# Seven scattered result areas replaced by two accumulating ones in a mixture-of-experts decoder layer

## The reference

```
N, k = 4096, 1024
scores = softmax(xt @ Wr)                      # token x expert
G, idx = top_k(scores.T, k)                    # each expert picks 1024 tokens
X_in = xt[idx]
h = gelu(einsum('ekd,edh->ekh', X_in, W1) + b1)
X_e = einsum('ekh,ehd->ekd', h, W2) + b2
contrib = G[..., None] * X_e
out = zeros((N, D)).at[idx].add(contrib)       # a token may be picked by several experts
x = layernorm(x + out)
```

## Time and profile before

| | |
|---|---|
| median of 3 runs | 586.69 us (585.83 to 591.93) |
| profiled execution | span 585.1 us, 11240 instructions (no time of its own is given beside the span) |
| TensorE busy | 94% of the span |
| VectorE, ScalarE, GpSimd busy | 71%, 56%, 44% |
| mean granted TensorE clock | 0.977 of full |
| HBM read, written | 36.85 MB, 26.08 MB |

### The profile page before, as it was taken

How to read it: one execution, slowest core, us unless ns; L and a number is a source line. 1 busy time by engine, 2 the same in 40 slices (tenths; PEclk the granted TensorE clock), 3 DMA queues, 4 the chain that set the end, 5 groups by cost and what they waited for, 6 DMA issues and landing times.

```text
span 585.1 us, 11240 instructions
## 1 busy us (share of the span) xinstructions
PE 549.5 (94%) x3477; PEld 427.6 (73%) x3477; DVE 417.1 (71%) x1051; ACT 327.3 (56%) x670; POOL 260.2 (44%) x368
## 2 busy tenths in 40 slices
PE   8999999999999999999999898998999999999880
PEld 7868787888888788788878676566676575668530
DVE  3686786787687688668877875788758845656753
ACT  3577776767777677776767543442333525443133
POOL 4123524434352443435243430002777777777732
PEclk9999999999999999999999998998999999999985
DMA  7033442232234023423312404900223443665652
GB/s 242 2 82 91 135 117 52 96 109 97 47 115 134 25 83 115 112 50 115 104 60 65 150 10 144 304 2 11 55 57 106 138 129 121 191 194 163 221 185 108
DMA packets 62151, 63.43 MB, mean 108 GB/s; under 512 B 11809, under 2 KB 48930, under 8 KB 61858
## 3 DMA queue, kind: packets, MB, share of 16 engines
q1 hardware_dynamic: 58096, 55.37, 30.8%
q0 software_dynamic: 3584, 7.58, 4.6%
q10 hardware_dynamic: 434, 0.02, 0.0%
HBM read 36.85 MB, written 26.08 MB: 108 GB/s over the span
## 4 chain that ended last, share of the span: by engine, by line
PE 77%; DVE 13%; ACT 4%; issue 2%; POOL 1%; DMA 1%; POOLq 0%; DVEq 0%; ACTq 0%
PE PS L1577 17%; PE PS L1635 10%; PE PS L1607 9%; PE PS L1908 8%; PE PS L1930 7%; PE PS L1623 5%; PE PS L1821 4%; PE PS L1831 4%; DVE pc L1395 2%; DVE csum L1158 1%; ACT shared L891 1%; DVE cmax L1147 1%; PE PS L1681 1%; PE PS L1675 1%; PE PS L1667 1%
## 5 line engine op out<-in xcount | busy, mean ns | idle before, releaser
L767 POOL TENSOR_TENSOR pn<-pc,crcp 128x512 f32<-128x512 f32 (+1 forms) x93 | 80.4, 891 | 69.3 <-DVE crcp L1161 69.3
L1035 ACT ACTIVATE shared<-PS,b1T 128x512 f32<-128x512 f32 x88 | 60.5, 687 | 85.7 <-PE PS L1821 49.5
L807 POOL DMA_INDIRECT shared<-table,idx x56 | 54.3, 970 | 64.5 <-DVE idx L1402 48.0
L1607 PE MATMUL PS<-shared,x1T 128*128 128x512 f32 (+1 forms) x192 | 72.4, 513 | 1.2 <-ACT x1T L906 1.0
L817 POOL DMA_INDIRECT spread<-pn,idx x56 | 62.0, 1107 | 17.6 <-issue 15.6
L1607 PEld LDWEIGHTS PS<-shared,x1T 128*128 128x128 f32 x192 | 35.0, 189 | 37.6 <-issue 35.2
L862 ACT ACTIVATE shared<-PS 128x308 f32<-128x308 f32 x120 | 47.5, 428 | 25.5 <-PE PS L1577 25.2
L1147 DVE TENSOR_REDUCE cmax<-PS 128x16 f32<-128x1232 f32 x31 | 44.7, 1441 | 20.8 <-PE PS L1607 20.4
L1158 DVE TENSOR_REDUCE csum<-pc 128x16 f32<-128x1232 f32 x31 | 44.4, 1431 | 19.4 <-ACT pc L874 19.4
L1908 PE MATMUL PS<-pT,w 128*128 128x512 f32 x112 | 53.6, 611 | 3.3 <-ACT pT L1030 3.3
L1930 PEld LDWEIGHTS PS<-w,shared 128*128 128x128 f32 x448 | 51.7, 192 | 3.6 <-issue 3.1
(11 more groups left out here) (209 smaller groups left out, 1208.1 us busy)
## 6 DMA issues: line engine op xcount, KB each, us to landing
spread<-zeros SPq DMA_DIRECT2D x112, 128.0 KB, 2.0
shared<-spread SPq DMA_DIRECT2D x56, 256.0 KB, 4.3
xboth<-in_x SPq DMA_DIRECT2D x16, 256.0 KB, 2.7
w<-in_W SPq DMA_DIRECT2D x2, 1792.0 KB, 9.2
rest<-stage SPq DMA_DIRECT2D x56, 52.0 KB
table<-x SPq DMA_DIRECT2D x16, 128.0 KB, 1.9
fin<-table SPq DMA_DIRECT2D x1, 2048.0 KB, 18.2
out_x<-fin SPq DMA_DIRECT2D x8, 256.0 KB, 2.0
```

The lines of the kernel that those rows point to most:

```text
L767: pool.tensor_tensor(pn[:, e, at_pn:at_pn + n * (b - a)].rearrange("p (h k) -> p h k", h=n), pc[:, e, :].rearrange("p (h k) -> p h k", h=H ...
L807: pool.indirect_dma_start(xg[:, e % 3, h, :], None, table, bass.IndirectOffsetOnAxis(ap=idx[:, e, h:h + 1], axis=0)).then_inc(gathered[e % ...
L1035: act.activation(hid[:, c, 512 * h:512 * h + 512], PS[:, HID_BANKS[k % len(HID_BANKS)], :], ACT.Gelu, bias=b1T[:, bias:bias + 1]).then_inc ...
L1607: i = pe.matmul(PS[:, n, 0:b - a], x1T[:, e, :], A[:, 2 * A_SLOT[phase] + e, a:b], start=True, stop=True)
```

## The change

Only two HBM areas remain, `spread[0]` and `spread[1]`. Even experts scatter to the first and odd ones to the second. Experts 0 and 1 overwrite cleared rows, as before; experts 2 to 6 use indirect DMAs that add to what the area holds (`compute_op=ALU.add`), and GpSimd waits before them until the scatters of expert e - 2, which went to the same area, have landed. SP clears two areas and loads two: `spread[1]` after the scatters of experts 1, 3 and 5, and `spread[0]` after those of 0, 2, 4 and 6, each part of it after the add of the same part of the first. VectorE adds eight parts, after `last_results`, in place of 48; TensorE takes in the second area by its identity matmuls.

```diff
+AREAS = 2
-        spread = [nc.dram_tensor(f"spread{e}", ...).ap() for e in range(LISTED)]
+        spread = [nc.dram_tensor(f"spread{e}", ...).ap() for e in range(AREAS)]
             def clear(q):
-                for e in range(LISTED):
+                for e in range(AREAS):
                     sp.dma_start(to_clear[e][q], zeros[:, :]).then_inc(cleared, 16)
...
-            for e in range(LISTED):
+            for e in range(LISTED - AREAS, LISTED):
                 sp.wait_ge(scattered[e % 2], 16 * SB * (e // 2 + 1))
-                rows = spread[e].rearrange("(t b) d -> t b d", t=P)
+                rows = spread[e % 2].rearrange("(t b) d -> t b d", t=P)
                 for c in range(B // 4):
-                    if e:
-                        sp.wait_ge(landed_added, B // 4 * (e - 1) + c + 1)
+                    if e == LISTED - 1:
+                        sp.wait_ge(landed_added, c + 1)
                     sp.dma_start(landed[:, 4 * c:4 * c + 4, :], rows[:, 4 * c:4 * c + 4, :]).then_inc(landed_in[c], 16)
...
             def scatter(e):
                 if e == 0:
-                    pool.wait_ge(cleared, 16 * LISTED * PAIRS)
+                    pool.wait_ge(cleared, 16 * AREAS * PAIRS)
+                if e >= AREAS:
+                    pool.wait_ge(scattered[e % 2], 16 * SB * (e // 2))
                 for h in range(SB):
                     pool.wait_ge(ye_done, blocks_through(e, h))
-                    pool.indirect_dma_start(spread[e], bass.IndirectOffsetOnAxis(ap=idx[:, e, h:h + 1], axis=0),
-                                            ye[:, e % 2, h, :], None).then_inc(scattered[e % 2], 16)
+                    rows = bass.IndirectOffsetOnAxis(ap=idx[:, e, h:h + 1], axis=0)
+                    if e < AREAS:
+                        pool.indirect_dma_start(spread[e % 2], rows, ye[:, e % 2, h, :], None).then_inc(scattered[e % 2], 16)
+                    else:
+                        pool.indirect_dma_start(spread[e % 2], rows, ye[:, e % 2, h, :], None,
+                                                compute_op=ALU.add).then_inc(scattered[e % 2], 16)
...
-            def dense_add(g, landed_before):
+            def dense_add(g):
-                if landed_before:
-                    dve.wait_ge(landed_added, landed_before)
...
-            def add_landed(e, first, last):
-                if e == 0 and first == 0:
-                    dve.wait_ge(fin_x, 16)
-                if added[0]:
-                    dve.wait_ge(dense_added, added[0])
-                for c in range(first, last):
-                    dve.wait_ge(landed_in[c], 16 * (e + 1))
-                    if e:
-                        dve.wait_ge(landed_added, B // 4 * (e - 1) + c + 1)
+            def add_landed():
+                dve.wait_ge(dense_added, added[0])
+                for c in range(B // 4):
+                    dve.wait_ge(landed_in[c], 16)
                     dve.tensor_tensor(fin[:, 4 * c:4 * c + 4, :], fin[:, 4 * c:4 * c + 4, :],
                                       landed[:, 4 * c:4 * c + 4, :], ALU.add).then_inc(landed_added, 1)
...
                 results(e, 0)
-                if e >= 2:
-                    add_landed(e - 2, 0, B // 8)
                 results(e, 1)
-                if e >= 2:
-                    add_landed(e - 2, B // 8, B // 4)
...
-            add_landed(LISTED - 3, 0, B // 4)
             last_results()
-            add_landed(LISTED - 2, 0, B // 4)
+            add_landed()
```

More of the change, by code:

```diff
@@ L456, in decoder_layer @@
         table = nc.dram_tensor("table", [TOKENS, ROW], F32, kind="Internal").ap()
-        spread = [nc.dram_tensor(f"spread{e}", [TOKENS, P], F32, kind="Internal").ap() for e in range(LISTED)]
+        spread = [nc.dram_tensor(f"spread{e}", [TOKENS, P], F32, kind="Internal").ap() for e in range(AREAS)]
         rest = nc.dram_tensor("rest", [PAIRS // PHASES, 2 * PHASES, HEADS, KEYS_REST, P], F32, kind="Internal").ap()
@@ L1479, in _ @@
                     make_idx(e + 3)
-                if e >= 2:
-                    add_landed(e - 2, 0, B // 8)
                 results(e, 1)
-                if e >= 2:
-                    add_landed(e - 2, B // 8, B // 4)
                 if e < 2:
                     for k in range(IN_ROUTING // 2 * e, IN_ROUTING // 2 * (e + 1)):
-                        dense_add(k, 0)
+                        dense_add(k)
                 if e - 1 in TAIL:
-                    dense_add(TAIL[e - 1], B // 4 * (e - 1))
-            add_landed(LISTED - 3, 0, B // 4)
+                    dense_add(TAIL[e - 1])
             last_results()
-            add_landed(LISTED - 2, 0, B // 4)
+            add_landed()
             def fin_shift(c):
@@ L1500, in fin_shift @@
                                          in1=rsf[:, 4 * c:4 * c + 4], op0=ALU.mult, op1=ALU.mult).then_inc(fin_shifted, 1)
-            dve.wait_ge(landed_added, B // 4 * (LISTED - 1))
+            dve.wait_ge(landed_added, B // 4)
             for c in range(B // 4):
@@ L1976, in _ @@
             for c in range(B // 4):
-                pe.wait_ge(landed_added, B // 4 * (LISTED - 2) + c + 1)
+                pe.wait_ge(landed_added, c + 1)
                 pe.matmul(PS[:, c, :], ident[:, :], fin[:, 4 * c:4 * c + 4, :].rearrange("p b d -> p (b d)"),
@@ L1980, in _ @@
             for c in range(B // 4):
-                pe.wait_ge(landed_in[c], 16 * LISTED)
+                pe.wait_ge(landed_in[c], 16 * AREAS)
                 pe.matmul(PS[:, c, :], ident[:, :], landed[:, 4 * c:4 * c + 4, :].rearrange("p b d -> p (b d)"),
```

## The result

The changed kernel takes 605.0 us (604.35 to 606.67) against 588.4 us of the kernel before in the same comparison: a ratio of 1.029, with an interval of 1.024 to 1.034. That is 3% slower, and outside the range that I gave.

The account below looks back on a forecast made before the run. TensorE, busy 94% of the span, covers most work; GpSimd's last scatters decide the gain. 2.2 - 0.6 - 1.2 = 0.4 us off a 585.1 us span gives 584.7, plus 1.6 to the median: 586.3 us, range 582.7 to 599.

Parts of the forecast that it names:

- part 3: 40 of 56 GpSimd scatters accumulate: 0.8 us on the path in the last two experts, 1.2 us covered before.
- d: Additional GpSimd issue time of one accumulating scatter: taken as 0.05 us, with bounds 0 and 0.97.
- cover of 2.1: Scatter issues beside VectorE adds, 2.1 us above bare earlier in the stage; their relief would hide 1.2 us of accumulating.
- rival (a): Slower through GpSimd's issue of accumulating scatters: 594 us at 0.3 us extra each, 621 at 0.97; chance 32%.
- All three signs: Forecast wrong if extra issue time exceeds 0.15 us, landings exceed 6 us, or TensorE waits for GpSimd's gathers.
- Part 1: 80 of 112 clears go in the attention stage, covered by TensorE: 0 us.
- Part 2: 40 of 48 landing adds go, 27.5 us of VectorE; shorter scatter issues in the tail gain 3.2 us.
- The rule that VectorE's adds lengthen issues: GpSimd scatters take 1.5 us beside VectorE adds with both inputs in SBUF, 0.96 to 0.97 us alone.
- The new wait: GpSimd waits before expert e's scatters for those of expert e - 2, issued a whole expert before: 0 us.
- Part 4: Landing of the last scatter: 0.6 us more for the accumulate's read, 1.2 us for a loaded queue.
- The 1.2 us for a loaded queue: Last scatter moves 2.2 us towards a saturated DMA queue, so its landing takes 1.2 us longer.
- Rival (b): Slower through the transfer: accumulates outlast the 1.27 us between issues and back up; about 592 us, chance 10%.

Follow-up runs that it names:

- experiment 1: Changed kernel with all scatters plain, none accumulating; 585.15 us, ratio 0.998 to the kernel before.
- experiment 5: Kernel before with VectorE's adds of expert 3 moved ahead of expert 5's results; 585.15 us against 586.17, ratio 0.997.
- experiment 2: Kernel before with 40, 16 (experts 5, 6) or 8 (expert 2) scatters accumulating, each into its own area; 608.85, 592.5 and 589.58 us.
- experiment 4: Changed kernel with fewer rows in the scatters of experts 0, 2, 3 and 4; 598.56 us in one run.

## Why the prediction was wrong

**The step that failed** is the one size in part 3: "I take 0.05, near the first end, because the two kinds in the trace differ so little". That put d at 0.05 us, and it measured 0.59: 23.6 us for the 40, where the sum had counted 0.8 on the path and hidden 1.2 under a cover of 2.1. That gather and scatter cost nearly the same says nothing of a third kind; I took the likeness of two known things as evidence on an unknown one, and then gave rival (a) 32% only, with the high end of the range at d = 0.43.

**The mechanism was the right one.** Rival (a) had the formula: the last issue ends at 553.4 + 16d + (24d - 2.1). With d = 0.59 it gives 574.9; measured are 576.5, or 574.4 with the 2.1 us of the later start taken off. At the start of expert 5's scatters it gives 24 x 0.59 - 2.1 = 12.1 us; measured 12.2. That this fits to 0.1 us is in part luck: the 24 issues came to 14.7 us above 24 x 0.97 and not 14.2, and the relief was larger than 2.1 by as much, since the five rows that I had summed were not all that were longer than bare (483.85, 485.25 and 509.37 took 1.10, 1.20 and 1.07). The point from which the change loses, d near 0.09 to 0.15, stood in the text, and the measured price is four to six times that. All three signs that I had named showed: d above 0.15, landings above 6 us, and TensorE's waits for gathers.

**Part 1** (clears, 0 us): right, by experiment 1.

**Part 2** (27.5 us of VectorE off the path, 3.2 us at the last issue): right as to the issue (553.8 against 553.4), incomplete in what follows. With the last issue 2.8 us earlier the chain went through TensorE's first group of identity matmuls. The prediction had left its pace alone, because TensorE idled between its two groups; in experiment 1 that idle time, 2.2 us before, is gone, and of the 2.8 us the median kept 1.3.

**The rule that VectorE's adds lengthen issues** held for plain scatters (0.98 against 1.49 us at the same place, experiment 5), and little for accumulating ones (0.5 us over 16 issues, experiment 2). Nor does it hold for each issue: two beside the adds of 521.17 to 523.68 in the kernel before took 0.98 and 0.97 us, and of six beside the block of adds in experiment 5 one took 1.50 and the others 0.97 to 0.99. What decides which one is lengthened stays open. I had not foreseen that the two prices overlap; the changed kernel has few adds, so it did not matter for it.

**The new wait** cost nothing, as said: GpSimd shows no idle time before its scatters in the changed kernel.

**Part 4** (landing, 0.6 + 1.2 us): counted from the start of the last issue, the landing grew by 0.8 us. The issue itself is 0.3 us longer (1.56 against 1.26), so 0.5 are left behind it, near the 0.6 that I gave the read; that they are the read isn't shown. The 1.2 us for a loaded queue did not come, since the last scatter was issued at 574.95, when the load of the other area had ended (VectorE's last add of it starts at 574.17). The 542.9 us given for the end of the odd experts' scatters doesn't follow from 532.60 and 1.27 us a scatter, which gives 542.5; nothing else hung on it.

**Rival (b)**, a transfer longer than the issue interval: no. The 40 accumulates landed after 3.3 us in the median, and up to 562 us all of them after 3.2 to 3.6 us, without a backlog. The longest took 7.0 us (6.2 in the kernel before), between 562 and 570, beside the load of the other area.

**The Trainium skill**, "Collectives: The Full Stack", in "Why ReduceScatter is half of AllGather", with two read descriptors for an add where a copy needs one, pointed to the right side, but the case that I had set beside it, an issue that doubles (621 us), was too high: the issue grew by 0.59 us on 0.97, and by experiment 4 most of that does not grow with the rows.

## What to carry to other kernels

Where an engine's rows lie back to back with only the fixed gap, it has little or no slack, whatever its share of busy time on the page (44% here, before the change): price every instruction on it first, and let the unknown price of a new kind of instruction set the range, not the likeness of the known kinds. If the forecast turns at a price (here 0.1 us) that lies deep inside the bounds of what is unknown (0 to 0.97), the forecast has no sign yet. Accumulating scatters save VectorE's adds only where GpSimd has time to give; here they took 24 us off an engine with slack and put 18 us on one with none.

## What the runs showed of the hardware

- An accumulating indirect DMA of 128 rows of 512 bytes takes GpSimd 1.56 us to issue, a plain scatter 0.97, a gather 0.94. With 64, 32 and 16 rows the accumulating one takes 1.40, 1.30 and 1.28 us, the plain one with 64 rows 0.90.
- The packet counts fit one packet for each row of an accumulate. The software queue had 3584 packets in the kernel before, 32 for each of 112 indirect DMAs. It had 4480 with 8 accumulates among them, 5376 with 16 and 8064 with 40: 112 more for each, so 144, which is 128 rows and 16. The kernel with fewer rows fits too (5888), if a plain scatter of 64 rows has 32 packets like one of 128.
- The HBM figures of a page do not show what an accumulate reads: with seven areas it is 36.85 MB read and 26.08 MB written, with 40 accumulating scatters as without.
- Beside adds of VectorE with both inputs in SBUF some plain scatters took 1.5 us to issue and others still 0.97. Accumulating ones beside such adds mostly stayed at 1.55, but 1.76 to 2.06 us also occurred (both in experiment 2: the kernels with 16 and with 40).
